# Attention and six local-attention layers on one core: dense keys with 64-row, 32-column score products, statistics by sequence, first loads and first weight products moved

## What is computed

```
A:  q, k, v = xn @ w_qkv (16 heads of 64); q, k normalized
    softmax(q k^T * scale) @ v over all 512 keys;  @ w_out + b_out
F:  six times
      x = local_attention(shift(x)) + x      # rotary q, k; windows of 32, 64 keys a query
      x = ffn(shift(x)) + x                  # layer norm, 128 -> 2 x 341, gelu gate, -> 128
```

## Time and profile before

| | |
|---|---|
| three runs | 4590.09, 4593.01, 4592.19 us; median 4592.19 |
| the profiled execution | 4594.7 us, its span 4592.9 us |
| share of the span busy | PE 95%, DVE 85%, PE weight loads 66%, ACT 65%, POOL 61% |
| mean granted TensorE clock | 0.991 |
| bytes over the span | 119.39 MB, 26 GB/s |

### The profile page before, as it was taken

How to read it: one execution, slowest core, us unless ns; L and a number is a source line. 1 busy time by engine, 2 the same in 40 slices (tenths; PEclk the granted TensorE clock), 3 DMA queues, 4 the chain that set the end, 5 groups by cost and what they waited for, 6 DMA issues and landing times. The chain is left out here.

```text
span 4592.9 us, 102400 instructions
## 1 busy us (share of the span) xinstructions
PE 4344.7 (95%) x36584; PEld 3036.2 (66%) x36584; DVE 3911.2 (85%) x5311; ACT 2982.6 (65%) x4227; POOL 2810.1 (61%) x4591
## 2 busy tenths in 40 slices
PE   5999999999899999999999999999999999999997
PEld 3555455555467777777777777777777777777775
DVE  6888788888688988898888899888988889989994
ACT  4666666666456676666666667666667667667663
POOL 3555555555466666666665666666666666666672
PEclk9999999999999999999999999999999999999998
DMA  1000000000110101101011111111011110111010
GB/s 53 3 6 5 3 5 3 5 3 3 33 43 22 31 24 34 48 25 30 26 40 40 27 28 32 45 27 33 24 33 47 27 31 25 28 52 27 26 30 14
DMA packets 256467, 119.39 MB, mean 26 GB/s; under 512 B 118336, under 2 KB 251456, under 8 KB 255168
## 3 DMA queue, kind: packets, MB, share of 16 engines
q1 hardware_dynamic: 256192, 115.87, 9.2%
HBM read 86.31 MB, written 16.91 MB: 22 GB/s over the span
## 5 line engine op out<-in xcount | busy, mean ns | idle before, releaser
L580 POOL TENSOR_TENSOR pn<-es,rden 128x1024 f32<-128x1024 f32 x192 | 366.6, 1909 | 779.1 <-DVE rden L915 779.1
L564 POOL TENSOR_TENSOR t<-t,ardn 128x1024 f32<-128x1024 f32 x256 | 485.1, 1895 | 304.1 <-DVE ardn L800 303.8
L674 ACT ACTIVATE y<-ps 128x1024 f32<-128x1024 f32 x384 | 372.2, 1021 | 349.6 <-PE ps L1116 349.6
L665 ACT ACTIVATE t<-ps,anm,srn 128x512 f32<-128x512 f32 x512 | 392.9, 771 | 271.1 <-DVE anm L809 271.1
L584 POOL TENSOR_TENSOR t<-t 128x1024 f32<-128x1024 f32 x192 | 454.7, 2368 | 85.1 <-DVE t L867 85.1
L867 DVE TENSOR_TENSOR t<-ps,tabl 128x512 f32<-128x512 f32 x768 | 490.1, 679 | 0.0
L865 DVE TENSOR_TENSOR t<-ps,tabl 128x1024 f32<-128x1024 f32 x384 | 466.5, 1215 | 16.8 <-ACT sq L690 13.3
L954 DVE TENSOR_REDUCE mx<-ps 128x16 f32<-128x1024 f32 x192 | 235.1, 1225 | 259.0 <-PE ps L1238 255.4
L586 POOL TENSOR_TENSOR t<-t 128x1024 f32<-128x1024 f32 x192 | 452.9, 2359 | 2.7 <-DVE t L867 2.7
L964 DVE TENSOR_TENSOR qn<-t,rn 128x2048 f32<-128x2048 f32 x192 | 437.9, 2281 | 5.8 <-POOL rn L389 5.8
L925 DVE TENSOR_REDUCE ss<-sq 128x32 f32<-128x2048 f32 x192 | 436.4, 2273 | 0.0
(11 more groups left out here) (136 smaller groups left out, 9329.5 us busy)
## 6 DMA issues: line engine op xcount, KB each, us to landing
xw<-tokens_dram SPq DMA_DIRECT2D x768, 64.0 KB, 1.9
tokens_dram<-x SPq DMA_DIRECT2D x96, 128.0 KB
xs<-tokens_dram SPq DMA_DIRECT2D x192, 64.0 KB, 1.9
xsh<-x SPq DMA_DIRECT2D x48, 128.0 KB
xsh<-x SPq DMA_DIRECT2D x48, 127.0 KB
wm<-in_l_wqk SPq DMA_DIRECT2D x3, 1024.0 KB, 4.9
wv<-in_l_wv SPq DMA_DIRECT2D x6, 512.0 KB, 3.9
wo<-in_l_wo SPq DMA_DIRECT2D x6, 512.0 KB, 5.4
```

The source lines that it names most:

```text
L564: nc.gpsimd.tensor_tensor(eA[:, v], eA[:, v], ardn[:, v].unsqueeze(2).to_broadcast([P, 2, SEQ]), ALU.mult).then_inc(a_pn, 1)
L665: e = act.activation(eA[:, j, h], bank(j % 2 * 2 + h), ACT.Exp, bias=anm[:, j, h:h + 1], scale=srn[:, a % 2, j, h:h + 1], accum_out=aden[: ...
```

## The change

- **Keys.** kpad becomes `kbuf`; kT in it is dense, 8 pairs by 544 positions, the two heads of a pair on rows 0 to 63 and 64 to 127. One copy of 128 rows fills it. POOL clears only its first 32 positions per pair.
- **Scores.** A product now takes 64 rows (one head) by 32 columns and streams 64 keys: 64 products a turn instead of 32. Even heads go to the first half of pool1, odd ones to the second, so heads lie in the order of `slot`, and L1176 needs no reordering.
- **Statistics by sequence.** The loop over all sequences and `rsqrt` go. `token_statistics(b+1)` stands in period 2, step 1, `token_guess(b+1)` in period 2, step 3, the 12 Newton steps on POOL in period 3.
- **First loads.** Sequence 0 comes first, then constants and the dense attention's weights, then the other sequences, the tables last; each user waits for its own.
- **First folding.** Layer 0's wv and wo are loaded at the start into xw, which is free until the layers; the products stand in the last batch's period 8, ACT copies them there. The wait for accd moves to turn (0, 3).

```diff
         wqkA = wqkL[0].rearrange("p (a c) -> p a c", a=PAIRS)
+        kT = kbuf[:, 0:PAIRS * (WIN + SEQ)].rearrange("p (a c) -> p a c", a=PAIRS)
+        wv0, wo0 = (a.rearrange("p u w d -> p (u w d)") for a in (xw[:, 0:2], xw[:, 2:4]))
         eA = t12[:].rearrange("p (j s k) -> p j s k", j=NU, s=2)
...
         def fold_part(s):
-            if s.static and s.b == -1:
-                return 0, 0, s.c
             if s.static and not s.last and (s.b, s.c) in FOLD:
                 return s.l + 1, 1 - s.v, FOLD[s.b, s.c]
             return None
...
+            def load_tokens(b, done):
+                sp.dma_start(acc[:, b * SEQ:(b + 1) * SEQ].rearrange("p (k d) -> p k d", k=NU),
+                             x_dram[:, b * NU:(b + 1) * NU, :]).then_inc(done, 16)
+            load_tokens(0, s_x0)
             sp.dma_start(cst[:], consts[:, 0:CST]).then_inc(s_ld, 16)
+            sp.dma_start(wqkL[0], a_wqk).then_inc(s_wa, 16)
+            sp.dma_start(wv[:].rearrange("p h d -> p (h d)"), a_wv).then_inc(s_wa, 16)
+            sp.dma_start(boutb[:], a_bout.partition_broadcast(P)).then_inc(s_ld, 16)
             sp.dma_start(sc[:], a_logit.partition_broadcast(P)).then_inc(s_ld, 16)
-            sp.dma_start(boutb[:], a_bout.partition_broadcast(P)).then_inc(s_ld, 16)
-            sp.dma_start(tab[:].rearrange("p a b c d -> p (a b c d)"), consts[:, CST:]).then_inc(s_ld, 16)
-            for b in range(NB):
-                sp.dma_start(acc[:, b * SEQ:(b + 1) * SEQ].rearrange("p (k d) -> p k d", k=NU),
-                             x_dram[:, b * NU:(b + 1) * NU, :]).then_inc(s_ld, 16)
+            sp.dma_start(wo[:].rearrange("p h d -> p (h d)"), a_wo).then_inc(s_wa, 16)
+            for b in range(1, NB):
+                load_tokens(b, s_x)
+            sp.dma_start(tab[:].rearrange("p a b c d -> p (a b c d)"), consts[:, CST:]).then_inc(s_tb, 16)
...
-            sp.dma_start(wqkL[0], a_wqk).then_inc(s_wa, 16)
-            sp.dma_start(wv[:].rearrange("p h d -> p (h d)"), a_wv).then_inc(s_wa, 16)
-            sp.dma_start(wo[:].rearrange("p h d -> p (h d)"), a_wo).then_inc(s_wa, 16)
...
             def turn(s):
                 c, t = s.c, s.t
+                if s.turn_of(-1, 1):
+                    sp.wait_ge(s_m, NU)
                 if s.turn_of(-1, 2):
...
                                                     ALU.mult).then_inc(a_pn, 1)
+                        if a == 3 and not last:
+                            if j == 0:
+                                pool.wait_ge(a_xg, b + 2)
+                            newton(pool, a_xr, b + 1, frn[:], fhalf[:], frt[:], range(3 * j, 3 * j + 3))
                         if a == 5 and j == 0 and not last:
                             copy_batch(b + 1)
+            pool.wait_ge(a_xg, 1)
+            newton(pool, a_xr, 0, frn[:], fhalf[:], frt[:])
             copy_batch(0)
             all_batches(pool, attend)
             pool.wait_ge(a_acc, NB * PAIRS)
-            nc.gpsimd.memset(kpad[:], 0.0).then_inc(s_zero, 1)
+            nc.gpsimd.memset(kT[:, :, 0:WIN], 0.0).then_inc(s_zero, 1)
             def turn(s):
...
+                        if last and a == PAIRS:
+                            act.wait_ge(s_m, j + 1)
+                            act.activation(mhL[0][:, j * 4:(j + 1) * 4].rearrange("p h d -> p (h d)"), bank(j),
+                                           ACT.Copy).then_inc(s_msb, 1)
...
                     act.wait_ge(l_tk, t + 3)
-                    act.activation(*keys(0, (c + 2) % NU), ACT.Copy)
-                    act.activation(*keys(1, (c + 2) % NU), ACT.Copy).then_inc(l_kT, 1)
+                    u = (c + 2) % NU
+                    act.activation(kT[:, :, WIN + u * P:WIN + (u + 1) * P], pool2.rearrange("p (a c) -> p a c", a=PAIRS),
...
-            with dve.Fori(0, NB) as b:
+            def token_statistics(b):
+                if isinstance(b, int):
+                    dve.wait_ge(s_x0, 16)
                 for u in range(NU):
-                    if u == 0:
-                        dve.wait_ge(a_mvc, at("a_mvc", b))
                     stat = nc.vector.bn_stats(st[:, u], acc[:, bass.ds(b * SEQ + u * P, P)])
                 stat.then_inc(a_st, 1)
                 dve.wait_ge(a_st, b + 1)
-                nc.vector.memset(rt[:, 0:NU], 0.0)
+                nc.vector.memset(gap[:], 0.0)
                 for u in range(NU):
                     stat = nc.vector.bn_aggr(agg[:, u], st[:, u])
                 stat.then_inc(a_mv, 1)
-                dve.wait_ge(a_mv, at("a_mv", b + 1))
-                nc.vector.tensor_copy(mv[:, bass.ds(b * NU, NU)], agg[:]).then_inc(a_mvc, 1)
-            dve.wait_ge(a_mvc, at("a_mvc", NB))
-            rsqrt((mv[:, :, 1], av[:]), rstd[:], artmp[:], 0, ALU.add, EPS)
-            dve.wait_ge(s_rs, RS)
...
+            def token_guess(b):
+                dve.wait_ge(a_mv, b + 1)
+                nc.vector.tensor_scalar(fhalf[:], agg[:, :, 1], EPS, 0.5, ALU.add, ALU.mult).then_inc(a_hv, 1)
+                dve.wait_ge(a_hv, b + 1)
+                nc.vector.tensor_scalar(frn[:].bitcast(I32), fhalf[:].bitcast(I32), -0.5, float(0x5F3759DF - (1 << 22)),
+                                        ALU.mult, ALU.add).then_inc(a_xg, 1)
...
-                nc.vector.tensor_tensor(heads(xnn, NU), heads(tokens, NU),
-                                        mv[:, bass.ds(b * NU, NU), 0:1].to_broadcast([P, NU, DIM]), ALU.subtract).then_inc(a_dev, 1)
+                nc.vector.tensor_tensor(heads(xnn, NU), heads(tokens, NU), agg[:, :, 0:1].to_broadcast([P, NU, DIM]),
+                                        ALU.subtract).then_inc(a_dev, 1)
                 dve.wait_ge(a_dev, b + 1)
-                nc.vector.tensor_tensor(heads(xnn, NU), heads(xnn, NU),
-                                        rstd[:, bass.ds(b * NU, NU)].unsqueeze(2).to_broadcast([P, NU, DIM]),
+                dve.wait_ge(a_xr, (b + 1) * RS_POOL)
+                nc.vector.tensor_tensor(heads(xnn, NU), heads(xnn, NU), frn[:].unsqueeze(2).to_broadcast([P, NU, DIM]),
...
+                        if a == 2 and j == 1 and not last:
+                            token_statistics(b + 1)
+                        if a == 2 and j == 3 and not last:
+                            token_guess(b + 1)
                         if a == 4 and j == 1 and not last:
                             normalize_tokens(b + 1)
+            token_statistics(0)
+            token_guess(0)
+            dve.wait_ge(s_ld, 16 * 3)
             normalize_tokens(0)
...
             all_batches(dve, attend)
...
-            def fold(n, q):
-                pe.wait_ge(s_wvo, (n + 1) * 32)
+            def products(q, a, b, to_bank):
                 for h in range(H):
                     to = slot(h)
                     if to // 4 == q:
                         rows = slice(h % 2 * DH, (h % 2 + 1) * DH)
-                        m = nc.tensor.matmul(ps_x[:, to % 4 * DIM:(to % 4 + 1) * DIM], wv[rows, h // 2], wo[rows, h // 2],
+                        m = nc.tensor.matmul(to_bank[:, to % 4 * DIM:(to % 4 + 1) * DIM], a[rows, h // 2], b[rows, h // 2],
                                              start=True, stop=True)
                 m.then_inc(s_m, 1)
...
+            def fold(n, q):
+                pe.wait_ge(s_wvo, n * 32)
+                products(q, wv, wo, ps_x)
+            def fold_first(q):
+                pe.wait_ge(s_wv0, 32)
+                pe.wait_ge(a_e, NB * STEPS - (q < 2))
+                products(q, wv0.rearrange("p (h d) -> p h d", h=PAIRS), wo0.rearrange("p (h d) -> p h d", h=PAIRS), bank(q))
...
                             m.then_inc(a_o, 1)
+                        if last and a == PAIRS:
+                            fold_first(j)
...
                     for a in range(PAIRS):
-                        for w in range(NW):
-                            key0 = u * P + w * WIN
-                            m = nc.tensor.matmul(pool1[w * WIN:(w + 1) * WIN, a * 2 * KEYS:(a + 1) * 2 * KEYS],
-                                                 qT[:, a, w * WIN:(w + 1) * WIN], kpad[:, 2 * a:2 * a + 2, key0:key0 + KEYS],
-                                                 start=False, stop=True, skip_group_check=True)
+                        for odd in range(2):
+                            rows = slice(odd * DH, (odd + 1) * DH)
+                            for w in range(NW):
+                                key0 = u * P + w * WIN
+                                m = nc.tensor.matmul(pool1[w * WIN:(w + 1) * WIN, odd * 512 + a * KEYS:odd * 512 + (a + 1) * KEYS],
+                                                     qT[rows, a, w * WIN:(w + 1) * WIN], kT[rows, a, key0:key0 + KEYS],
+                                                     start=False, stop=True, skip_group_check=True)
...
+            pe.wait_ge(s_avg, 1)
+            pe.wait_ge(s_mask, 2)
+            pe.wait_ge(s_row, 2)
+            pe.wait_ge(s_msb, NU)
```

(5 more changed lines are left out.)

64 lines of the change are left out of this document (26 added, 38 removed).

## The result

The changed kernel took 4542.49 us (median of four runs, 4540.59 to 4543.85) against 4592.6 us before in the same session: ratio 0.9891, 95% interval 0.9874 to 0.9908. That is 50 us faster. The forecast was 4442, the likeliest case 4422 to 4465; the whole range, to 4565, holds the time, but the gain is a third of the 150 us forecast. The profiled execution's span is 4538.8 us against 4592.9.

What follows compares the result with a forecast made beforehand. PE was taken to set the pace in the layers (busy 65.55 of 67.10 us a batch). Scores -121, start -25.5, statistics +6, passage -10: 4594.7 - 150.5 - 2.5 = 4442 us; range 4422 to 4565, likeliest 4422 to 4465.

Steps and rivals of the forecast that it cites:

- the likeliest case: Whole kernel: all terms about as worked out, 4422 to 4465 us; chance 0.64.
- the term of the scores: Layers' score products: 16 rounds of 0.058 us gain 0.80 us a turn in 151 turns, -121 us.
- My own sign of being wrong: Layers: score block not shorter than 1.4 us, or DVE's wait before the maximum gone in turns other than c=0.
- The overlap of the halves: Layers' score block: all eight tiles run at the same time, so a round of eight takes 0.058 us.
- Rival A: Layers' score block: halves overlap in part, a round takes 0.080 us, gain 0.47 a turn, 4492 us; chance 0.13.
- Rival C: New score block: PE cannot start records faster than 0.027 us apart, 128 take 3.5 us, 4888 us; chance 0.07.
- my +6: Dense attention: statistics of seven sequences inside DVE's loop cost 0.85 us each, +6 us, between 0 and 13.
- In c=0 shorter scores buy nothing: First turn of a layer batch: ACT's chain behind the table load binds; 39 of 190 turns cannot gain.
- c=1 and c=3: Second and fourth turns of a layer batch: 15.55 us instead of 16.35, though 17.15 for c=1.
- The start: Before the first matmul: PE starts at 11.7 us instead of 37.25, -25.5 us, 3 less if a load is late.
- The passage: Between attention and layers: less clearing and earlier folding bring the first projection forward, -10 us, between -4 and -14.
- The first projection was to run 33 us earlier: Sign at the beginning of the layers: their first projection 33 us or so earlier than before the change.

Runs made afterwards that it cites:

- experiment 6: Changed kernel with each of the 64 score products streaming 32 keys in place of 64: 4522.15 us.
- experiment 2: Changed kernel with the statistics of sequences 1 to 7 all in the first batch, outside DVE's loop: 4533.16 us.
- experiments 2 to 4: experiment 2, then no_scores_c0, then short_by_64 and short_by_128, each the changed kernel with one edit: 4533.16, 4540.19, 4557.59 and 4520.56 us.
- short_by_64: Changed kernel with 16 of the 64 score products left out in turns c=0, 64 PE instructions a batch less: 4557.59 us.
- no_scores_c0: Changed kernel with 63 of the 64 score products left out in turns c=0: 4540.19 us.
- experiment 7: Changed kernel with one extra one-element gelu ahead of ACT's feed-forward wait in turns c=0, so the table loads early: 4513.82 us.
- Experiment 1: Kernel before with only the dense keys and the new 64-row, 32-column scores: 4564.84 us.
- best2: Changed kernel with statistics in the first batch, early table load, two small loads ahead of the weights, and ACT's qT copy in two halves: 4442.34 us.
- short_by_128: Changed kernel with 32 of the 64 score products left out in turns c=0, 1702 PE loop instructions a batch: 4520.56 us.

## Why the prediction was wrong

**What failed first: the term of the scores was mis-sized.** "A burst costs some 0.007 us a record. With eight tiles a burst needs about 0.055 us ... I take 0.058 for a round". The 0.007 came from bursts of four that followed 0.089 us of pause. Measured, 16 rounds take 1.27 us, a mean of 0.080 a round, so the gain was 0.47 us a turn (c=2: 16.35 to 15.89) and not 0.80. The cost of a round was right for the first four (0.056, experiment 6) and was carried on to all sixteen, where no row showed such starts kept up; the other 96 records went 0.0101 us apart. My own sign of being wrong, a score block not shorter than 1.4 us, came true (1.49). The overlap of the halves was right, as their order showed (1.89 us in place of 1.49 without it). Rival A has the measured 0.080 and with it 4492, but not the reason: it blamed halves that overlap in part, and in the first rounds they overlap fully. Its number was luck. Rival C, a limit at the mean distance of before (0.027), is out: the mean is 0.010. By the rule of the Trainium skill that I weighed (TensorE: Matmul & The Clock Gate, "Wait — 56ns, not 53.3ns?") starts would lie 25 ns apart; for these tiles the measurement decides against it.

**What failed second: a cost that was not in the sum.** I counted the products' records and their stream, but not their room in the loop. Between rival A's 4492 and the measured 4542 lie 50 us, and 45 of them are in the layers: by 0.47 us a turn 71 would have been gained there, and 26.3 were. For PE's loop the profile has 28.6 us of "issue" ahead of L1009, and the turn c=0 grew by up to 1.4 us where it should have stayed; the rest, some 16 us, lies mainly in c=1 and c=3. In the attention DVE's loop cost 12 us (experiment 2); my +6, put there for another reason, hid half of it. That loading is the cause is shown by experiments 2 to 4, best by the passes of one copy of the loop with and without blocks. The page of before could have warned me: the earlier trace rows and the loads of q8 only outside the repeated batches showed that bodies stay on the chip, and a body two fifths longer is a reason to ask whether it still would.

**c=0.** "In c=0 shorter scores buy nothing" was right: passes without loads have c=0 at 16.1 to 16.4 us, whether 48 products stand in it (short_by_64) or one (no_scores_c0). But taking the 39 turns as bound by ACT for good hid a gain: the table load of 1.28 us behind the 2.93 us wait, worth 29 us in the changed kernel, was in the rows I quoted.

**c=1 and c=3** were forecast to gain like c=2. They gave 12.6 and 11.0 us in all, half of c=2's 20.6. In c=1 a part is the wait for xT one turn earlier: with it gone, c=1 takes 17.18 us for 17.79 (experiment 7). In c=3 DVE's wait is up to 1.56 us where c=2 has 1.25, so something ahead of the scores was late by 0.3 in part of these turns. Experiment 1 shows the same; the cause in c=3 was not tried.

**The start** missed by 2 us: the roots ended at 8.8, earlier than the 9.6 worked out, and the small load behind the weights, of which I had said "3 less if a load is late", held DVE until 13.28. The weights, which I had put at 10, would have held PE until 14.88 anyway (best2). **Statistics in the loop**: by the steps 0.2 us a batch and not 0.85 (my two terms, 0.4 and 0.4, add up to 0.8); the +9.5 of this stretch comes from the loop's edge, so the sign and size fit for a wrong reason, which is luck. **The passage** came out as worked out. The first projection was to run 33 us earlier and ran 20.3 earlier; the 33 had left out my own +6, and the attention lost more than that.

The forecast of 4442 for the changed kernel and the 4442 that best2 took have nothing to do with each other.

## What to carry to other kernels

When a change adds instructions to a loop, count the loop's body and not only the work: look at the queues of instruction loads and at the first instruction behind the loop's edge for a wait that "issue" ended. Price a new rhythm of small products by a sustained run of them: here the first 32 records of a block went at the pace of the burst, and the other 96 did not. And before making a block shorter, follow the wait of each engine ahead of it: here a table load ahead of its wait and a copy in two halves brought 95 us on the old kernel, nearly twice the change itself, for a few lines each.

## What was unexpected of the hardware

- A body of 323 program instructions on DVE made it wait 3.37 us where its loop went back; one of 311, 0.53 us.
- On PE a body of about 1830 instructions (some 885 products and as many weight loads in a batch, and some 60 more) was loaded in every pass, by some nine blocks of 16 KB; about 1578 was not; 1766 and 1702 were loaded in some passes and not in others, even of the same copy of the loop. A pass with loads began with a wait of 0.7 to 2.8 us.
- An idle time of 1.79 to 1.88 us ahead of L1131 was followed by a granted clock of 0.50 in 21 of 38 cases; idle times of 0.6 us (changed kernel) and 1.23 us (short_by_128) were not.
- 64-row, 32-column products over eight tiles start 0.0067 us apart within the first round, go on at 0.056 us a round of eight up to the 32nd record with 64 columns streamed, and then at 0.0101 us a record (0.0088 with 32 columns).
